# Inverse norms of queries and keys by logarithm, exponential and one Newton step, two chunks at a time, in a two-layer attention and MLP kernel

## What is computed

```python
def l2norm(t):
    return t / jnp.clip(jnp.linalg.norm(t, axis=-1, keepdims=True), 1e-12)

def _layer(x, wqkv, qs, ksc, wo, lg, lb, w1, b1, w2, b2):
    h = shift_token(x)
    q, k, v = jnp.split(h @ wqkv, 3, axis=-1)      # then to 8 heads of 64
    q = l2norm(q) * qs
    k = l2norm(k) * ksc
    q, k = rotary_xpos(q, k)
    o = local_attention(q, k, v)                   # windows of 64 tokens and the 64 before
    x = x + o.reshape(b, n, INNER) @ wo
    h = shift_token(x)
    h = (h - mu) / jnp.sqrt(var + 1e-05) * lg + lb
    a, g = jnp.split(h @ w1 + b1, 2, axis=-1)
    return x + (a * jax.nn.gelu(g, approximate=False)) @ w2 + b2

for l in range(2):
    x = _layer(x, ...)
```

## Time and profile before

| | us |
|---|---|
| median of three runs | 1306.38 |
| lowest, highest | 1305.3, 1306.8 |
| profiled execution | 1305.02 |
| its span | 1303.2 |
| first scores of stage F (PE) | 590.65 |

### The profile page before, as it was taken

How to read it: one execution, slowest core, us unless ns; L and a number is a source line. 1 busy time by engine, 2 the same in 40 slices (tenths; PEclk the granted TensorE clock), 3 DMA queues, 4 the chain that set the end, 5 groups by cost and what they waited for, 6 DMA issues and landing times.

```text
span 1303.2 us, 37200 instructions
## 1 busy us (share of the span) xinstructions
PE 1200.7 (92%) x12352; PEld 984.2 (76%) x12352; DVE 1124.0 (86%) x2210; ACT 958.8 (74%) x1772; POOL 1070.0 (82%) x1431
## 2 busy tenths in 40 slices
PE   3799999999999999977899999999999999999975
PEld 2588888888888888865677777777777777777764
DVE  2799999999999999957888888888888988888873
ACT  3477777777777777655688878888887877787762
POOL 1877777777777777687999999999999999999962
PEclk9799999999999999998999999999999999999998
DMA  6000000000000000001121211112122111111110
GB/s 181 8 12 14 14 14 14 12 12 12 9 11 12 12 8 10 16 7 46 40 48 39 49 42 43 46 46 50 39 53 52 45 50 47 49 48 47 43 35 25
DMA packets 87053, 44.28 MB, mean 34 GB/s; under 512 B 43908, under 2 KB 80048, under 8 KB 86960
## 3 DMA queue, kind: packets, MB, share of 16 engines
q1 hardware_dynamic: 86960, 43.08, 12.9%
HBM read 19.99 MB, written 6.29 MB: 20 GB/s over the span
## 4 chain that ended last, share of the span: by engine, by line
PE 39%; POOL 32%; DVE 14%; issue 11%; SPq 2%; ACT 1%; POOLq 1%; DVEq 0%; DMA 0%; ACTq 0%
POOL rnorm L716 11%; POOL kT L705 9%; PE bank L1415 7%; PE bank L1382 6%; PE bank L1397 6%; POOL probs L766 4%; DVE sums L1083 4%; POOL kT L719 3%; PE bank L1357 3%; DVE probs L1100 2%; PE bank L1426 2%; PE bank L1533 2%; PE bank L1359 2%; PE bank L1512 2%; PE bank L1568 2%
## 5 line engine op out<-in xcount | busy, mean ns | idle before, releaser
L655 POOL TENSOR_TENSOR probs<-probs,coef 128x1024 f32<-128x1024 f32 x128 | 241.0, 1904 | 5.0
L716 POOL TENSOR_TENSOR rnorm<-norm,halves 128x8 f32<-128x8 f32 x128 | 213.8, 1671 | 10.7
L705 POOL TENSOR_TENSOR kT<-qT 128x512 f32<-128x512 f32 x128 | 164.0, 1281 | 7.2 <-DVE qT L1177 7.2
L1091 DVE TENSOR_REDUCE mx<-bank 128x8 f32<-128x512 f32 x256 | 162.8, 678 | 3.9 <-PE bank L1397 3.8
L1100 DVE TENSOR_TENSOR probs<-bank,mx 128x512 f32<-128x512 f32 x256 | 162.1, 675 | 0.1
L849 ACT ACTIVATE probs<-probs 128x1024 f32<-128x1024 f32 x128 | 135.2, 1056 | 35.7 <-DVE probs L1100 33.8
L1083 DVE TENSOR_REDUCE sums<-probs 128x16 f32<-128x1024 f32 x128 | 154.0, 1212 | 6.5 <-ACT probs L849 6.5
L1382 PE MATMUL bank<-ident,probs 128*128 128x128 f32 x1024 | 137.8, 278 | 10.1 <-ACT wT L843 7.4
L719 POOL TENSOR_TENSOR kT<-kT,rnorm 128x512 f32<-128x512 f32 x128 | 133.6, 1044 | 10.0
L843 ACT ACTIVATE wT<-bank 128x512 f32<-128x512 f32 x256 | 137.1, 589 | 0.5 <-PE bank L1382 0.5
L1382 PEld LDWEIGHTS bank<-ident,probs 128*128 128x128 f32 x1024 | 114.2, 142 | 26.0 <-issue 14.2
(11 more groups left out here) (130 smaller groups left out, 3107.8 us busy)
## 6 DMA issues: line engine op xcount, KB each, us to landing
probs<-f_v SPq DMA_DIRECT2D x96, 128.0 KB, 2.3
res<-stage_x SPq DMA_DIRECT2D x48, 128.0 KB, 3.8
xn<-in_x SPq DMA_DIRECT2D x16, 128.0 KB, 2.2
xr<-in_x SPq DMA_DIRECT2D x16, 128.0 KB, 2.1
stage_x<-xo SPq DMA_DIRECT2D x32, 64.0 KB, 1.6
hn<-stage_x SPq DMA_DIRECT2D x32, 64.0 KB
mn<-mid SPq DMA_DIRECT2D x64, 32.0 KB
stage_x<-yo SPq DMA_DIRECT2D x16, 128.0 KB, 2.1
```

The lines of the kernel that those rows point to most:

```text
L655: nc.gpsimd.tensor_tensor(out=e[:, :, :, :], in0=e[:, :, :, :], in1=coef[r % 2][:, 2, A_REP * at:A_REP * (at + 1), :].unsqueeze(3).broadca ...
L705: nc.gpsimd.tensor_tensor(out=qk[m][:, :, :], in0=on_self[m % 2][:, :, :], in1=on_partner[m % 2][:, :, :], op=ALU.add).then_inc(added, 1)
L716: nc.gpsimd.tensor_tensor(out=rnorm[:, at], in0=norm2[:, 1, at], in1=halves[:, 0:F_HEADS], op=ALU.pow).then_inc(rnorm_set, 1)
L1091: nc.vector.tensor_reduce(mx[s % 2][:, 2 * k:2 * k + 2, :], banks[2 * (s % 2) + k][:, :].rearrange("p (h c k) -> p h c k", h=2, c=CHUNKS), ...
```

## The change

For the inverse roots:
- ACT squares with scale 2, so that norm2 is four times the sum of squares, and the floor is four times as high.
- POOL takes the max once for two chunks (128x16), at the end of a step.
- At the start of the next step ACT takes the logarithm of it and the exponential of -0.5 times that: root[:, 1], half of the inverse length, near. Both functions are in one table set, which is loaded by hand behind the gelus, at the start of an odd step; the scores' exponential uses the same set, and no other load stands before it. There are as many loads in a turn as before.
- POOL makes one Newton step of four small instructions, root x root, times norm2, three less that, times root, each with a wait for the one before, and then the two large products of the two chunks (`normalise`, at the start of the step and in front of the first sum).

And for the transposes: on PE the first of a step lies behind the weighted values, and the second behind the values' matmul v; ACT's copies go in the same order, foT first.

```diff
@@ POOL @@
-                def normalise(unit, m):
-                    ...
-                    nc.gpsimd.tensor_scalar_max(norm2[:, 1, at], norm2[:, 0, at], NORM_FLOOR).then_inc(guarded, 1)
-                    pool.wait_ge(guarded, index + 1)
-                    wait(pool, qk_normed, index - 3)
-                    nc.gpsimd.tensor_tensor(out=rnorm[:, at], in0=norm2[:, 1, at], in1=halves[:, 0:F_HEADS], op=ALU.pow).then_inc(rnorm_set, 1)
...
+                def guarded_norms(index, tile):
+                    at = slice(2 * F_HEADS * tile, 2 * F_HEADS * (tile + 1))
+                    pool.wait_ge(consts_set, N_CONSTS)
+                    pool.wait_ge(norm_step, index + 1)
+                    nc.gpsimd.tensor_scalar_max(norm2[:, 1, at], norm2[:, 0, at], 4.0 * NORM_FLOOR).then_inc(guarded, 1)
+
+                def normalise(unit, tile):
+                    at, j = slice(2 * F_HEADS * tile, 2 * F_HEADS * (tile + 1)), TILES * unit + tile
+                    k = ROOT_STEPS * j
+                    pool.wait_ge(root_near, j + 1)
+                    pool.wait_ge(guarded, j + 1)
+                    nc.gpsimd.tensor_tensor(out=root[:, 2, at], in0=root[:, 1, at], in1=root[:, 1, at], op=ALU.mult).then_inc(root_step, 1)
+                    pool.wait_ge(root_step, k + 1)
+                    nc.gpsimd.tensor_tensor(out=root[:, 2, at], in0=root[:, 2, at], in1=norm2[:, 1, at], op=ALU.mult).then_inc(root_step, 1)
+                    pool.wait_ge(root_step, k + 2)
+                    nc.gpsimd.tensor_tensor(out=root[:, 2, at], in0=threes[:, 0:2 * F_HEADS], in1=root[:, 2, at], op=ALU.subtract).then_inc(root_step, 1)
+                    pool.wait_ge(root_step, k + 3)
+                    wait(pool, qk_normed, 2 * (j - TILES) + 2)
+                    nc.gpsimd.tensor_tensor(out=rnorm[:, at], in0=root[:, 2, at], in1=root[:, 1, at], op=ALU.mult).then_inc(root_step, 1)
+                    pool.wait_ge(root_step, k + 4)
+                    for m in range(2 * tile, 2 * tile + 2):
+                        pool.wait_ge(added, 4 * unit + m + 1)
+                        nc.gpsimd.tensor_tensor(out=qk[m][:, :, :], in0=qk[m][:, :, :],
+                                                in1=rnorm[:, F_HEADS * m:F_HEADS * (m + 1)].unsqueeze(2).broadcast_to([P, F_HEADS, F_HD]),
+                                                op=ALU.mult).then_inc(qk_normed, 1)
@@ POOL, body @@
+                        if prepares(turn, p, tile) and not (turn == "first" and s == 0):
+                            normalise(unit + tile, 1 - tile)
                         if prepares(turn, p):
                             sums(4 * (unit + 1) + 2 * tile, 2 * tile)
-                            normalise(unit + 1, 2 * tile)
...
                         if prepares(turn, p):
                             sums(4 * (unit + 1) + 2 * tile + 1, 2 * tile + 1)
-                            normalise(unit + 1, 2 * tile + 1)
+                            guarded_norms(4 * (unit + 1) + 2 * tile + 1, tile)
@@ ACT @@
-                    nc.scalar.activation(sq[m % 2][:, :], f_bank("qk", local, turn)[:, :], ACT.Square).then_inc(squared, 1)
+                    nc.scalar.activation(sq[m % 2][:, :], f_bank("qk", local, turn)[:, :], ACT.Square, scale=2.0).then_inc(squared, 1)
...
+                def roots_near(unit, tile):
+                    at, j = slice(2 * F_HEADS * tile, 2 * F_HEADS * (tile + 1)), TILES * unit + tile
+                    act.wait_ge(guarded, j + 1)
+                    wait(act, root_near, j - 1)
+                    nc.scalar.activation(root[:, 0, at], norm2[:, 1, at], ACT.Ln).then_inc(log_set, 1)
+                    act.wait_ge(log_set, j + 1)
+                    wait(act, root_step, ROOT_STEPS * (j - TILES + 1))
+                    nc.scalar.activation(root[:, 1, at], root[:, 0, at], ACT.Exp, scale=-0.5).then_inc(root_near, 1)
@@ ACT, body @@
+                        if tile == 1 and f_exists(turn, s - 1, F_LATE["gates"]) and f_exists(turn, s):
+                            load_log_and_exp()
+                        if prepares(turn, p, tile) and not (turn == "first" and s == 0):
+                            roots_near(unit + tile, 1 - tile)
                         if tile == 1 and prepares(turn, p, 2):
                             rounded(it, p + 2, turn)
...
-                        if prepares(turn, p, tile):
-                            transposed(unit + tile, 4 * (p + tile) + 2 - 2 * tile, 2 - 2 * tile, turn)
...
                         if prepares(turn, p, tile):
-                            transposed(unit + tile, 4 * (p + tile) + 3 - 2 * tile, 3 - 2 * tile, turn)
+                            transposed(unit + tile, 4 * (p + tile) + 2 - 2 * tile, 2 - 2 * tile, turn)
                         if prepares(turn, p):
                             values_read(unit + 1, TILES * (p + 1) + tile, tile, turn)
+                        if prepares(turn, p, tile):
+                            transposed(unit + tile, 4 * (p + tile) + 3 - 2 * tile, 3 - 2 * tile, turn)
@@ PE, body @@
+                        if follows:
+                            weighted_values(it, late, late_s // TILES, late_s % TILES)
                         if prepares(turn, p, tile):
                             if follows:
                                 pe.wait_ge(eT_read, 2 * late + 2)
                             ahead("qkT", 4 * (p + tile) + 2 - 2 * tile)
-                        if follows:
-                            weighted_values(it, late, late_s // TILES, late_s % TILES)
                         following("values")
+                        if prepares(turn, p):
+                            ahead("v", TILES * (p + 1) + tile)
                         if prepares(turn, p, tile):
                             pe.wait_ge(f_read["qkT"], 4 * (unit + tile) + 3 - 2 * tile)
                             ahead("qkT", 4 * (p + tile) + 3 - 2 * tile)
-                        if prepares(turn, p):
-                            ahead("v", TILES * (p + 1) + tile)
```

More of the change, by code:

```diff
@@ L325, in build @@
         weights_rounded, weights_split, hT_rounded = sem("weights_rounded"), sem("weights_split"), sem("hT_rounded")
[L326 to L327 removed]
+        squared, norm_step, guarded, added, log_set, root_near, root_step, qk_normed = (
+            sem(n) for n in ("squared", "norm_step", "guarded", "added", "log_set", "root_near", "root_step", "qk_normed"))
         f_scored, f_max, f_sub, f_exp, f_sum_set, f_rsum_set, f_normed, f_divided, eT_made, eT_read = (
@@ L1178, in rotate @@
                                             tab(1).rearrange("p h (t d) -> p h t d", t=2), ALU.mult).then_inc(rotated, 1)
-                    wait(dve, guarded, 4 * before + m + 1)
+                    wait(dve, guarded, TILES * before + m // 2 + 1)
                     nc.vector.tensor_reduce(norm2[:, 0, F_HEADS * m:F_HEADS * (m + 1)],
```

26 lines of the change are left out of this document (16 added, 10 removed).

## The result

The changed kernel takes 1319.95 us, median of four runs (1317.12 to 1324.09), against 1306.59 us for the kernel before beside it: ratio 1.0106, 95% interval 1.0084 to 1.0128. It is slower by 13.4 us. Forecast were 1290.3 us, a range of 1280 to 1313, and 0.62 for faster; the time lies outside the range and on the other side. The profiled execution took 1318.74 us, its span is 1317.0.

The account below looks back on a forecast made before the run. POOL was taken to pace both layers, with PE close behind in layer 0. Handover -2.4, first seven steps -10.5, layer 0 +5.9, layer 1 -7.7 and last even step -1.3 made -16.0: 1290.3 us on the median, range 1280 to 1313.

Parts of the forecast that it names:

- POOL paces both layers: Kernel before: POOL sets units of 20.66 and 22.3 us; in layer 0 PE, busy 20.32, is the next bound.
- The collision: Odd steps, both layers: rival that POOL's large product blocks DVE's hc, +20.3 us, giving 1310.6; chance 0.34.
- decides below about 1.29 us: Collision rival: POOL's product blocks hc's second if it starts before about 1.29 us after ScalarE's exponential ends.
- a few hundredths: Argument against the collision: each POOL step with two waits adds this much, starting its product later and letting hc through.
- The price of 0.75: Collision rival's cost per unit in us, bounds 0.5 and 1.0, over 27 units.
- The low part's stall: Odd steps: DVE's low part waits for ScalarE's fhT_high behind the table load, 0.42 us in layer 0, 0.73 in layer 1.
- The even steps: "nothing": Even steps: logarithm and exponential fall in ScalarE's idle time, and moved transposes and copies have cover, so no cost.
- The copies of the keys "late for the scores": Rival: keys' copies not covered before the next scores, 0.5 us a step; named under something else slower, chance 0.04.
- the -10.5 forecast: First seven steps: 72.0 us shrink to 61.6 with POOL relieved; an estimate, bounds -4 and -13.
- The copies of eT: Odd steps: PE's weighted values, waiting for eT, come a good 1 us later but end before the down-projection's release.
- Residual of layer 1, last even step: DVE's 1.33 us wait for POOL's residual goes: layer 1 even steps 9.80 us, last even step -1.3.
- The handover from stage A: Stage start, PE idle until POOL sets the pads: shorter chunks, less ScalarE's stall, give -2.4 us (0 to -4).
- The load empties the engine: Rival: behind the gelus the table load also drains ScalarE, 1.28 us per odd step, +34.6, giving 1324.9; chance 0.04.

Follow-up runs that it names:

- run 5: Kernel before, with each chunk's power replaced by a product of the same 8 columns (inverse root left out): 1267.81 us, ratio 0.9707.
- run 8: Changed kernel plus one unread small POOL product between Newton step and large products, in odd steps with an hc: 1299.2 us, ratio 0.9946.
- Run 4: Kernel before, with only the transposes and their copies moved to the new order, power kept: 1305.88 us, ratio 1.0006.
- 6: Run 2's kernel (hc ahead of the low part), with transposes and copies in the order of before in even steps alone: 1284.92 us, ratio 0.9844.
- run 3: Changed kernel with the chunks' transposes and copies back in the order of before, on PE and ACT: 1322.79 us, ratio 1.0129.
- run 9: Changed kernel with ScalarE's rounding of fhT_high moved ahead of the table load, logarithm and exponential in odd steps: 1290.36 us, ratio 0.9887.
- run 10: Run 9's kernel with hc ahead of the low part and the old transpose order in even and the first four steps: 1280.44 us, ratio 0.9821.
- run 1: Changed kernel, but in odd steps POOL waits for hc before its two large products: 1298.06 us, ratio 0.9935.
- run 2: Changed kernel with DVE's hc moved ahead of the low part in odd steps: 1289.02 us, ratio 0.988.
- run 7: As 6, with the old transpose order also in all eight steps of the two written-out turns at the start: 1281.75 us, ratio 0.9813.
- run 11: Run 9's kernel with all transposes in the order of before: 1339.8 us, ratio 1.0257.

## Why the prediction was wrong

- **POOL paces both layers, and in layer 0 "the next bound is right behind".** Right: run 5 gains 2.1 us in layer 0 and 15.4 in layer 1. POOL's share fell to 69%, not 65%.
- **The collision.** This step failed. The sum left it out, and it had a chance of 0.34. A blocked hc is there in 29 of its 64 instructions: twice in the fifth step after the stage's first and once in each of the 27 odd steps that follow it. The starts themselves were worked out well. Counted from the end of the exponential, hc's first starts at 1.04 in the rows, as summed. In the nine written-out steps its second is at 1.29 and POOL's product at 1.28, inside the 1.26 to 1.33 of the sum: there the product blocks by the prediction's own rule. What failed is that rule for the others, that the product "decides below about 1.29 us" and that "a few hundredths" of POOL's waits let hc through. In the 18 loop steps those hundredths came (a wait of 0.18 in front of the fourth small product), the product began at 1.41, 0.08 behind the record of hc's second (1.33), and it blocked hc all the same. It takes between 0.08 and 0.16 to let hc through (run 8). Where a sum finds two starts closer than its own terms are known, neither side may be called the likelier. The price of 0.75 is right for the written-out steps (0.78) and short for the loop's (0.91). Together that is 9 x 0.78 + 18 x 0.91 = 23 us, and 1.6 more in the step with two.
- **The low part's stall**, 0.42 and 0.73 a step: measured 0.43 (written-out turns) or 0.52 (loop), and 0.66 in layer 1. Right, and its terms too: the load 1.28, and 0.45 from the logarithm to fhT_high, where 0.38 was summed (the wait between the two is 0.11, not 0.08, and each is 0.22 long). Layer 1 by the sum was 11.76 for an odd step; with the blocked hc it is 12.61.
- **The even steps: "nothing".** Wrong by 0.2 in a typical step of layer 0. PE's second transpose waits for ACT's copy of the first (in the unit at 800.61 the copy ends at 806.39 and the transpose starts at 806.52), as both use one bank. Run 4 shows it alone, 6 takes it back.
- **The copies of the keys "late for the scores"** had 0.04 as a rival, "0.5 a step". In the first seven steps it holds: 0.69 us in the row above, where no gates or down-projection cover the copy. Of the -10.5 forecast only 3.9 came; run 5 shows that 10.2 were to be had. Of the 6.3 between them, run 3, with the transposes of before, has 2.9 back (0.8 of that is one blocked hc less), and the blocked hc of two steps cost about 2. The rest stays open.
- **The copies of eT.** The prediction has PE's weighted values "a good 1 us later but still end before the down-projection is released". The copies come 1.65 us later (3.26 into the step, 1.61 before) and the weighted values 0.2 (4.40 and 4.19), since a transpose no longer stands ahead of them. They do end in time, but the products of the values, which stand behind them on PE and are waited for by DVE, come later too. Where no blocked hc covers that, in run 9, the odd steps are 0.15 to 0.36 longer than 11.03; that this is the reason was not tried by itself.
- **Residual of layer 1, last even step.** Right: even steps of 9.82 where 9.80 was summed, and -1.7 us for the last one where -1.3 was.
- **The handover from stage A**, -2.4: the profile has -2.1, and that is luck. Of ten profiles with the new roots only this one and run 10 reach the second step ahead of the 601.30 of the kernel before; the others are 0.6 to 2.2 us behind it, at a lower granted clock (see the hardware, below). Nor does the sum give -2.4 by its own terms: 17.3 - 13.7 is 3.6, no row shows the 13.7, and how much the stall of ScalarE takes off isn't worked out. The -2.8 us after the last step were not forecast either, and lie within the 6 us by which kernels with the same work differ there.
- **The load empties the engine.** Right to give it little. It starts 0.02 after the gelu and the logarithm 0.01 after it. The drain that the Trainium skill's "ScalarE: Activation LUTs", section "What ACT_TABLE_LOAD costs", adds to every switch is nowhere in these rows.

In one line: the removal was worth up to 38 us by the medians (run 5), and the profiled execution of run 5 is 49.4 us shorter than the changed kernel's. An estimate from the rows: 25 of these are the blocked hc, 15 the load's place in ACT's queue, and about 7 the moved transposes (3.7 in layer 0, 1.1 in layer 1, some 2 in the first seven steps).

## What to carry to other kernels

When work leaves an engine that paces, ask not only what it frees but what it now starts earlier, and beside which neighbour: here a large GpSimd product landed on a VectorE operation from SBUF to SBUF. If two such starts come out closer than 0.2 us, put the choice into the code (a wait, or the order of a queue) instead of guessing it; one instruction moved turned 1.1% slower into 1.1% faster. And a long instruction that is inserted ahead of a queue (a table load) belongs behind whatever another engine needs next.

## What the runs showed of the hardware

- An hc TENSOR_SCALAR, 0.34 us long alone, comes out 1.08 to 1.21 us long beside a POOL product of 1.04, and its record ends 0.08 behind the product's in every case. It is so for products that begin from 0.05 ahead of its record to 0.08 behind it (the 29 instructions of the changed kernel). From 0.16 behind it on, hc is not held; between 0.16 and 0.17 the product is, by 0.04 (run 8). The Trainium skill, "SBUF — State Buffer", section "SBUF: two separate sides", describes such an exclusion and gives it to the one that starts first. These runs agree with the exclusion; by the start times of the records, a product that begins 0.08 later still comes first. POOL's small products of 16 columns (0.22 us) made the hc beside them longer by 0.04 at most (0.37 for 0.33).
- TensorE's granted clock can fall within a step, to 0.53 over 3 us (run 3). That step is 1.3 us longer than one with the same waits at full clock.
- The granted clock also differs in the first step of the stage, behind a pause of PE, between kernels that have the same code up to that point. The same stretch of the changed kernel and of run 9:

```profile
575.00:593.00 18.00, 11.30 (x116) 9.27 (x117) 6.29 (x13) 8.42 (x21) 11.18 (x23) 1.00 0.09 23
593.00:602.00 9.00, 5.68 (x59) 3.77 (x57) 8.70 (x16) 5.98 (x15) 5.02 (x9) 1.00 0.30 76
```

```profile
575.00:593.00 18.00, 12.24 (x109) 10.38 (x109) 4.86 (x10) 6.95 (x17) 10.60 (x21) 0.81 0.03 9
593.00:602.00 9.00, 6.54 (x59) 4.17 (x51) 7.36 (x12) 4.70 (x9) 4.01 (x4) 0.79 0.41 104
```

At full clock the first step is 7.66 us long and the second begins at 599.2 (run 10, 599.05); at 0.78 to 0.81 the first is 9.0 to 9.1 long and the second begins at 601.9 to 603.5 (runs 1 to 3, 6 to 9 and 11). The kernel before had 0.87 there, and 7.66. These 3 us belong to no change; why one profile has them and another not stays open. Together with the stretch after the last step (40.3 to 46.4 us, granted clock 0.98 to 0.77), this is why two profiles are to be compared stretch by stretch and not by their ends.
